# Pair 1 of the row tiles by seven products, begun while Y's signed sums are still being made

## The chip, the cores and the metric

The kernel runs on one core of one Trainium2 chip. The metric is device time in microseconds, the median of three runs. A TensorE program, a VectorE, a ScalarE and a GpSimd program and a queue of transfers (SP, called the transfer queue below) run side by side and wait for one another through semaphores.

## What is computed

`x` has 4096 rows of 512, `adj` is a 4096 by 4096 matrix of zeros and ones. Two layers follow one another, each with a residual and a layer norm:

```python
x = _layernorm(x + _L0_gnn_ref(x, key, value, adj, ...))   # attention, masked by adj, over 4096 keys
x = _layernorm(x + _L1_gnn_ref(x, adj, W, b))

def _L1_gnn_ref(features, adj, W, b):
    agg = adj @ features
    out = jnp.einsum('nd,od->no', agg, W) + b
    return jax.nn.relu(out)
```

The first layer takes four fifths of the time and is not changed. The kernel reorders the second: it first makes Y = x1 W^T (4096 by 512, x1 the first layer's result) and then adj @ Y. Every fp32 number on TensorE is split into two fp16 halves, HI and LO; `adj` is exact in bf16, so adj @ Y needs two matmuls for each 128x128 block of `adj`, one with Y's HI and one with its LO.

## The kernel before

**Y.** The first layer finishes one tile of 128 rows at a time. `rows_product(n)` (TensorE, 12 matmuls, line 952) makes tile n of Y. It needs the turned x1 tile `x1T`, two transposing transfers from the transfer queue (L542, L545). Tiles 0 to 27 of Y go through DRAM and are loaded into the large tile `Y` by GpSimd's queue; the last four are written to it by ScalarE and VectorE (`last_y_high`, `last_y_low`).

**Row tiles by pairs.** The 32 row tiles of the output are made in 16 pairs: pair p is row tile p and row tile p + 16. For each, both strips of `adj` are brought in, transposed, as `AT[p % 2][0]` and `AT[p % 2][1]` (32 blocks of 128x128 each). For pairs 0 and 1 a strip comes in four parts (`adj_part`, L563), for the later ones at once (`adj_tile`, L569). `at_in[h][k]` counts the parts that have landed.

**Plain pairs and pairs by seven products.** Pairs below `PLAIN` = 2 are made plainly by `aggregate(p, k, m0, m1)` (L1024): 32 blocks times HI and LO, 64 matmuls of 512 columns for each strip, 128 for a pair, with the accumulator in PSUM bank `2 * (p % 2) + k`. The other 14 pairs see the pair as a 2 by 2 block matrix (strip k, left or right half of the 4096 columns), Y as 2 by 2 (upper or lower half of the rows, left or right 256 columns), and multiply them by Winograd's scheme of seven products instead of eight. `product` (L1057) is 16 matmuls of 512 columns (256 columns, HI and LO side by side), so a pair costs 7 x 16 = 112.

The scheme needs sums of both factors. VectorE makes four sums of the `adj` strips for each pair, `adj_sum(0..3)` (L2107, tiles `S12`, `S34`, semaphore `s_comb`); sum 0 is the sum of the two halves of strip 1, so it waits for both strips. The signed sums of Y are the same for all pairs (tiles `Ta`, `Tb`, 16 groups of four): groups 0 to 10 (`EARLY` = 11) are made during the second pass of the first layer, stored in DRAM as `ts_dram` and loaded at the end by GpSimd's queue (L782, semaphores `ts_ld`, 5.5 MB in three transfers). Groups 11 to 15 need the last tiles of Y and are made at the end by VectorE and ScalarE: `joined(m)` (L2031) adds HI and LO, `last_sums(m)` (L1823 to L1828) makes the four sums, `signed_high(m)` (ScalarE, L1391) and `signed_low(m)` (L2042) split them; `t_lo2` counts the groups that are complete.

**After the products.** VectorE adds the seven products up in eleven steps (`taken`, `together`, L2114 and L2119, semaphore `c_step`), then `output` (L2062 scales and adds the bias, L2066 takes the relu and adds the x1 tile `zf`, L2069 takes statistics) and `result` (the root, L1783 to L1792, and L2078), and GpSimd's queue stores the tile. ScalarE copies product 0 out of its bank. TensorE waits in `seven` for `c_step` of the pair before (`read`), since each product has one bank: 0, 1, 2, 3, 6, 5, 4.

**The order around the change.** It is written out by hand. TensorE interleaves the last `rows_product` calls with pieces of `aggregate(0, ...)` and `aggregate(1, 0, 0, 8)`, then finishes pair 0, then pair 1, and goes on with `seven` for pair 2. VectorE makes the groups 11 to 15, then the outputs of tiles (0,0), (0,1), (1,0), then the four `adj` sums of pair 2, then the output of (1,1). The transfer queue issues in this order: `x1T` of tile 31, the four parts of strip `AT[1][1]`, the two `zf` tiles of pair 0 (L682), and when pair 0 is aggregated the two strips of pair 2 (L569).

Of the kernel before, what the change touches and what calls it, by code (L numbers as in the profile page):

```python
# [50 lines left out]
def attention_then_aggregation(nc, x, x_t, adj, key_t0, key_t1, value, wq, bq, wk, bk, wv, bv, wm_t, bm, w1, b1, out):  # L51
# [3 lines left out]
    P = 128  # L55
    KD = D // P
    NT = N // P
# [9 lines left out]
    PLAIN = 2  # L67
# [26 lines left out]
    with ctx:  # L94
# [278 lines left out]
        with nc.Block() as block:  # L373

            @block.sync
            def _(sp):
# [312 lines left out]
                for p in range(NP):  # L689
                    if p + 2 < NP:  # L690

                        q = p - PLAIN
                        if q < 0:
                            sp.wait_ge(f_mm, 2 * (p + 1))
                        else:
                            sp.wait_ge(s_prod, 7 * q + 6)
                            sp.wait_ge(s_comb, 4 * (q + 1))
                        for k in range(2):
                            adj_tile(p + 2, k)
                    if p + 1 < NP:  # L700
                        for k in range(2):
                            load_row(p + 1, k)
# [112 lines left out]
            def _(pe):  # L815
# [195 lines left out]

                def aggregate(p, k, m0, m1):

                    bank = 2 * (p % 2) + k
# [27 lines left out]
                aggregate(1, 0, 0, 8)  # L1042
# [7 lines left out]
                aggregate(1, 0, 8, NT)  # L1050
                aggregate(1, 1, 0, NT)

                def product(bank, left, right):
                    for m in range(NP):
                        last = nc.tensor.matmul(ps[:, bank, :].rearrange("p (s d) -> p s d", s=2), left(m), right(m),  # L1057
                                                start=(m == 0), stop=(m == NP - 1))
                    last.then_inc(s_prod, 1)

                def upper(h):
                    return lambda m: Y[:, m, :, h * H:(h + 1) * H]

                def lower(h):
                    return lambda m: Y[:, NP + m, :, h * H:(h + 1) * H]

                def signed(i):
                    return lambda m: (Ta, Tb)[m // PT2][:, m % PT2, i, :, :]

                def adj_block(h, k, half):  # L1070
                    return lambda m: AT[h][k][:, NP * half + m, :]

                def adj_sum(i):
                    return lambda m: (S12, S34)[i // 2][:, i % 2, m * P:(m + 1) * P]

                def seven(q, h, turn):
                    def read(step):

                        if not isinstance(q, int) or q > 0:
                            pe.wait_ge(c_step, 11 * (q - 1) + step)  # L1080

                    def plain_out(bank):

                        if isinstance(q, int) and q == 0:
                            pe.wait_ge(f_out, bank + 1)

                    pe.wait_ge(at_in[h][0], 16 * (turn + PARTS))
                    if not isinstance(q, int) or q > 0:
                        pe.wait_ge(s_cp, q)
                    plain_out(0)  # L1090
                    product(0, adj_block(h, 0, 0), upper(0))
                    read(1)
                    plain_out(1)
                    product(1, adj_block(h, 0, 1), lower(0))
                    pe.wait_ge(s_comb, 4 * q + 1)
                    if isinstance(q, int) and q == 0:
                        for c in range(3):
                            pe.wait_ge(ts_ld[c], 16)
                        pe.wait_ge(t_lo2, NP)
                    read(4)  # L1100
                    plain_out(2)
# [3 lines left out]
                    plain_out(3)  # L1105
# [10 lines left out]

                for p in range(PLAIN, PLAIN + 2):
                    seven(p - PLAIN, p % 2, p // 2)
# [303 lines left out]
            def _(dve):  # L1422
# [636 lines left out]
                def output(u, k, src, stored):  # L2059
# [3 lines left out]
                                                   op0=ALU.mult, op1=ALU.add).then_inc(f_out, 1)  # L2063
                    dve.wait_ge(zf_in[k], 16 * (stored + 1))
# [16 lines left out]
                def plain_output(p, k):  # L2081
                    u = 2 * p + k
                    dve.wait_ge(f_mm, u + 1)
                    output(u, k, ps[:, 2 * (p % 2) + k, :], p)
                    result(u, k)

                dve.wait_ge(s_bm, 32)
                plain_output(0, 0)
                plain_output(0, 1)
                plain_output(1, 0)  # L2090
# [3 lines left out]
                def adj_sum(i, q, h, turn):  # L2094
# [8 lines left out]
                    if q is not None:  # L2103
                        dve.wait_ge(s_prod, 7 * q + used)
# [4 lines left out]
                for i in range(4):  # L2109
                    adj_sum(i, None, PLAIN % 2, PLAIN // 2)  # L2110
                plain_output(1, 1)
# [10 lines left out]
                def pair(q, h, turn, nxt):  # L2122
# [9 lines left out]
                    dve.wait_ge(s_prod, 7 * q + 4)  # L2132
# [5 lines left out]
                    dve.wait_ge(s_prod, 7 * q + 5)  # L2138
# [4 lines left out]
                    dve.wait_ge(s_prod, 7 * q + 6)  # L2143
# [4 lines left out]
                    output(u, 1, cs[:, 1, :], q + PLAIN)  # L2148
# [3 lines left out]
                    dve.wait_ge(s_prod, 7 * q + 7)  # L2152
# [3 lines left out]
                    output(u + 1, 0, cs[:, 0, :], q + PLAIN)  # L2156
# [4 lines left out]
                for p in range(PLAIN, PLAIN + 2):  # L2161
                    pair(p - PLAIN, p % 2, p // 2, ((p + 1) % 2, (p + 1) // 2))
# [111 lines left out]
```

## Time and profile before

| what | value |
|---|---|
| median of 3 runs | 2019.56 us (2019.53 to 2020.5) |
| the profiled execution's own time | 2023.72 us |
| its span, first to last instruction | 2022.1 us |
| TensorE busy, of the span | 2003.9 us, 99% |
| VectorE busy | 1457.9 us, 72% |
| ScalarE busy | 689.6 us, 34% |
| mean granted TensorE clock | 0.999 |
| matmuls | 9273 |

The profiled execution is one execution under the hardware profiler, with a time of its own. Times within it are counted from the first instruction. The stretch that the change touches lies between about 1629 us and 1700 us. In a row of the timeline, the first number is the start, the second the time from there to the end of the last instruction of the row. Matmuls overlap, so the length of a row of n matmuls is longer than n times their distance; distances are taken from one start to the next.

### The profile page before, as it was taken

What the parts mean: (1) busy time and instruction counts of PE and PEld (TensorE: products, weight loads), DVE (VectorE), ACT (ScalarE), POOL (GpSimd) and SP (SyncE); (2) the same over time, 40 slices, a digit from 0 to 9 for tenths busy, and PEclk for the clock granted to TensorE, in tenths of its full rate; (3) what the DMA queues carried; (4) which work ended last, traced back from release to release, by engine and by line L of the source; (5) the groups of instructions that cost most, each with busy time, mean ns of one, the idle gap of its engine ahead of it and who ended that gap; (6) DMA issues with size and microseconds to landing.
All of it is one profiled execution on the core that took longest, in us unless ns stands there. A gap on an engine that the chain in (4) does not pass through costs nothing.

```text
span 2022.1 us, 29159 instructions
## 1 busy us (share of the span) xinstructions
PE 2003.9 (99%) x9273; PEld 920.8 (46%) x9273; DVE 1457.9 (72%) x3378; ACT 689.6 (34%) x859; POOL 72.1 (4%) x127
## 2 busy tenths in 40 slices
PE   8999999999999999999999999999999999999998
PEld 6444444444444444444444444444444444444443
DVE  7875666656666666777777777788888658788887
ACT  6854343434444443433333333344443210000000
POOL 0100000000000000000000000000000000000000
PEclk9999999999999999999999999999999999999999
DMA  8667778677777778877766676677777996555551
GB/s 296 229 167 157 202 176 207 151 157 166 179 175 176 187 165 206 197 165 167 166 162 161 164 166 161 164 168 178 182 184 208 220 274 146 125 128 137 133 134 60
DMA packets 566263, 351.22 MB, mean 174 GB/s; under 512 B 483520, under 2 KB 487616, under 8 KB 564288
## 3 DMA queue, kind: packets, MB, share of 16 engines
q1 hardware_dynamic: 548416, 279.26, 55.3%
q0 software_dynamic: 17792, 71.31, 15.3%
q8 instruction: 25, 0.41, 0.1%
q14 instruction: 30, 0.25, 0.0%
HBM read 176.95 MB, written 88.60 MB: 131 GB/s over the span
## 4 chain that ended last, share of the span: by engine, by line
PE 97%; SPq 1%; DVE 1%; DMA 1%; ACT 1%; issue 0%; DVEq 0%; ACTq 0%
PE ps L917 32%; PE ps L897 32%; PE ps L1057 17%; PE ps L874 4%; PE ps L952 4%; PE ps L938 4%; PE ps L1024 2%; PE ps L831 1%; SPq L563 1%; PE ps L849 1%; PE ps L819 0%; DMA PT<-Phl 0%; ACT prob L1243 0%; DVE prob L1685 0%; SPq L426 0%
## 5 line engine op out<-in xcount | busy, mean ns | idle before, releaser
L917 PE MATMUL ps<-V,PT 128*128 128x512 f16 x3072 | 673.5, 379 | 1.8 <-issue 1.4
L897 PE MATMUL ps<-KT,thl 128*128 128x512 f16 x3072 | 673.1, 379 | 0.0
L917 PEld LDWEIGHTS ps<-V,PT 128*128 128x128 f16 x3072 | 300.5, 98 | 364.6 <-issue 2.7
L897 PEld LDWEIGHTS ps<-KT,thl 128*128 128x128 f16 x3072 | 300.6, 98 | 362.1
L1672 DVE SCALAR_TENSOR_TENSOR prob<-ps,c_now,adjh 128x512 f32<-128x512 f32 x256 | 191.8, 750 | 264.1 <-PE ps L897 262.6
L1238 ACT ACTIVATE small<-prob 128x512 f32<-128x512 f32 x256 | 161.1, 630 | 621.1 <-DVE prob L1672 335.7
L1701 DVE SCALAR_TENSOR_TENSOR Phl<-prob,Phl 128x2048 f16<-128x2048 f32 x64 | 146.6, 2290 | 73.4 <-ACT Phl L1251 73.2
L1685 DVE CUSTOM_DVE_ANT_0 prob<-prob,small 128x512 f32<-128x512 f32 x256 | 174.2, 682 | 0.0
L1243 ACT ACTIVATE prob<-prob,nbias,inv 128x2048 f32<-128x2048 f32 x64 | 134.0, 2095 | 98.1 <-DVE nbias L1694 98.1
L1678 DVE TENSOR_SCALAR small<-small,eps_s,neg_s 128x512 f32<-128x512 f32 x256 | 138.7, 542 | 20.7 <-ACT small L1238 20.6
L1251 ACT ACTIVATE Phl<-prob 128x2048 f16<-128x2048 f32 x64 | 122.3, 1910 | 7.1
L1414 ACT ACTIVATE p<-ps 128x512 f32<-128x512 f32 x14 | 8.4, 597 | 323.5 <-PE ps L1057 323.5
L1057 PE MATMUL ps<-Y,AT 128*128 128x512 f16 x448 | 99.0, 379 | 0.0
L938 PE MATMUL ps<-Wvm,UT 128*128 128x512 f16 x384 | 88.1, 379 | 1.6 <-DMA UT<-Uhl 1.6
L952 PE MATMUL ps<-W1T,x1T 128*128 128x512 f16 x384 | 88.1, 379 | 0.2 <-DMA x1T<-x1hl 0.2
L758 POOL DMA_DIRECT2D adjh<-in_adj x64 | 36.8, 575 | 1364.3 <-DMA adj_bf<-adjh 701.1
L874 PE MATMUL ps<-xT,Aq 128*128 128x512 f16 x384 | 84.0, 379 | 0.0
L1057 PE MATMUL ps<-Ta,S 128*128 128x512 f16 x336 | 79.4, 379 | 0.0
L1057 PE MATMUL ps<-Tb,S 128*128 128x512 f16 x336 | 79.4, 379 | 0.0
L1057 PEld LDWEIGHTS ps<-Y,AT 128*128 128x128 bf16 x448 | 43.8, 98 | 52.9
L938 PEld LDWEIGHTS ps<-Wvm,UT 128*128 128x128 f16 x384 | 37.5, 98 | 47.2 <-DMA UT<-Uhl 2.1
L952 PEld LDWEIGHTS ps<-W1T,x1T 128*128 128x128 f16 x384 | 37.4, 98 | 46.1 <-DMA x1T<-x1hl 1.2
(205 smaller groups left out, 1677.3 us busy)
## 6 DMA issues: line engine op xcount, KB each, us to landing
adjh<-in_adj POOLq DMA_DIRECT2D x64, 512.0 KB, 5.3
adj_bf<-adjh SPq DMA_DIRECT2D x64, 512.0 KB, 4.7
t_in<-t_dram SPq DMA_DIRECT2D x64, 256.0 KB, 3.4
x_in<-in_x SPq DMA_DIRECT2D x64, 256.0 KB, 4.6
xraw<-in_x_t SPq DMA_DIRECT2D x8, 1024.0 KB, 7.3
t_dram<-tq POOLq DMA_DIRECT2D x8, 1024.0 KB, 5.5
o_dram<-z_out SPq DMA_DIRECT2D x32, 256.0 KB, 2.8
o_in<-o_dram SPq DMA_DIRECT2D x32, 256.0 KB, 4.5
```

The lines of the kernel that those rows point to most:

```text
L874: last = nc.tensor.matmul(ps[:, BT + e, :], Aq[:, m, k, e * P:(e + 1) * P], xT[:, b, s, k, :], start=(n == 0), stop=(n == 3 * KD - 1))
L897: last = nc.tensor.matmul(ps[:, BS + c, :], thl[:, b, s, k * P:(k + 1) * P], KT[:, m, k, c * C:(c + 1) * C], start=(n == 0), stop=(n == 3 ...
L917: last = nc.tensor.matmul(ps[:, BU + b, :], PT[:, b, s, m, :], V[:, v, m, :], start=(m == 0 and q == 0), stop=(m == MT - 1 and q == 2))
L938: last = nc.tensor.matmul(ps[:, BZ, :], UT[:, b, s, k, :], Wvm[:, m, k, :], start=(n == 0), stop=(n == 3 * KD - 1))
L952: last = nc.tensor.matmul(ps[:, BY, :].rearrange("p (o n) -> p o n", n=P), x1T[:, s, k, :], W1T[:, m, :, k, :], start=(q == 0), stop=(q == ...
L1057: last = nc.tensor.matmul(ps[:, bank, :].rearrange("p (s d) -> p s d", s=2), left(m), right(m), start=(m == 0), stop=(m == NP - 1))
L1238: nc.scalar.activation(small[:, c % 2, :], prob[:, b, c * C:(c + 1) * C], ACT.Abs).then_inc(s_abs, 1)
L1243: nc.scalar.activation(prob[:, b, :], prob[:, b, :], ACT.Exp, bias=nbias[:, b:b + 1], scale=inv[:, half:half + 1], accum_out=rsum[:, b:b + ...
L1672: nc.vector.scalar_tensor_tensor(out=prob[:, b, c * C:(c + 1) * C], in0=ps[:, BS + c, :], scalar=c_now[:, b:b + 1], in1=adjh[:, b, c * C:( ...
L1678: nc.vector.tensor_scalar(small[:, c % 2, :], small[:, c % 2, :], eps_s[:, half:half + 1], neg_s[:, half:half + 1], ALU.is_lt, ALU.mult).t ...
L1685: nc.vector.tensor_tensor_reduce(out=prob[:, b, c * C:(c + 1) * C], in0=prob[:, b, c * C:(c + 1) * C], in1=small[:, c % 2, :], scale=1.0, ...
L1701: nc.vector.scalar_tensor_tensor(out=Phl[:, b, LO, :], in0=prob[:, b, :], scalar=P_SCALE, in1=Phl[:, b, HI, :], op0=ALU.mult, op1=ALU.subt ...
```

## The change

`PLAIN` becomes 1, so pair 1 is made by seven products too, with an order of its own, and the other pairs keep theirs. On TensorE `aggregate(1, ...)` is gone. In its place stand product 0 of pair 1 (its first 8 matmuls ahead of the last `rows_product`), product 1, then product 4 (sum 3 of the strips times the lower part of Y), none of which needs Y's signed sums, then groups 0 to 10 of products 2, 3, 6 and 5, and at last groups 11 to 15 of the same four. Pair 0 now accumulates in banks 2 and 3. On VectorE the `adj` sums of pair 1 and the first step of pair 0's outputs (`take`, the bias step, which frees the banks) come between group 13 and group 14 of Y's sums, and the rest of pair 0's outputs after group 15. The transfer queue's instructions are the same; the third wait of its loop over pairs is another one.

```diff
-    PLAIN = 2
+    PLAIN = 1
...
-                            sp.wait_ge(s_prod, 7 * q + 6)
+                            sp.wait_ge(s_prod, 7 * q + (7 if q == 0 else 6))
...
-                    bank = 2 * (p % 2) + k
+                    bank = 2 + k
...
-                aggregate(1, 0, 0, 8)
+
+                pe.wait_ge(at_in[1][0], 16 * PARTS)
+                product(0, adj_block(1, 0, 0), upper(0), 0, NP // 2)
                 rows_product(NT - 1)
...
-                aggregate(1, 0, 8, NT)
-                aggregate(1, 1, 0, NT)
...
+                product(0, adj_block(1, 0, 0), upper(0), NP // 2, NP)
+                product(1, adj_block(1, 0, 1), lower(0))
+                pe.wait_ge(s_comb, 3)
+                pe.wait_ge(u_mg, NT)
+                product(4, adj_sum(3), lower(1))
+                for c in range(3):
+                    pe.wait_ge(ts_ld[c], 16)
+
+                pe.wait_ge(f_out, 1)
+                product(2, adj_sum(0), signed(0), 0, EARLY)
+                pe.wait_ge(f_out, 2)
+                product(3, adj_sum(1), signed(1), 0, EARLY)
+                pe.wait_ge(s_comb, 4)
+                pe.wait_ge(s_z, NT)
+                product(6, adj_sum(2), signed(2), 0, EARLY)
+                pe.wait_ge(at_in[1][1], 16 * PARTS)
+                product(5, adj_block(1, 1, 1), signed(3), 0, EARLY)
+                pe.wait_ge(t_lo2, NP)
+                product(2, adj_sum(0), signed(0), EARLY, NP)
+                product(3, adj_sum(1), signed(1), EARLY, NP)
+                product(6, adj_sum(2), signed(2), EARLY, NP)
+                product(5, adj_block(1, 1, 1), signed(3), EARLY, NP)
...
-                for m in range(EARLY + 2, NP):
-                    joined(m)
-                    signed_low(m - 2)
-                    last_sums(m)
-                signed_low(NP - 2)
-                signed_low(NP - 1)
...
+                joined(EARLY + 2)
+                signed_low(EARLY)
+                last_sums(EARLY + 2)
+                for i in (0, 1, 3, 2):
+                    adj_sum(i, None, PLAIN % 2, PLAIN // 2)
+                dve.wait_ge(s_bm, 32)
+                for k in range(2):
+                    dve.wait_ge(f_mm, k + 1)
+                    take(k, ps[:, 2 + k, :], 0)
+                for m in range(EARLY + 3, NP):
+                    joined(m)
+                    signed_low(m - 2)
+                    last_sums(m)
+                signed_low(NP - 2)
+                signed_low(NP - 1)
+                for k in range(2):
+                    output(k, k, 0)
+                    result(k, k)
```

Here `adj_sum(i, ...)` with i = 0 waits for both strips, `at_in[1][0]` and `at_in[1][1]`, before it starts. In the step that combines the products of pair 1 the counts of `s_prod` are moved by one (`made_at`), since product 4 is made third.

TensorE, the end of pair 0 and pair 1. Before, 16 matmuls of `aggregate(1, 0)` stand ahead of the last Y product and the other 112 of pair 1 behind pair 0's (the last 64 of them, strip 1, are the first two rows here); the products of pair 2 follow:

```order
L1024 MATMUL ps<-Y,AT 128x512 [waits adj_pair1_tile1_in]
L1024 MATMUL ps<-Y,AT 128x512 x63
L1057 MATMUL ps<-Y,AT 128x512 [waits aggregate_out,adj_pair0_tile0_in]
L1057 MATMUL ps<-Y,AT 128x512 x15
L1057 MATMUL ps<-Y,AT 128x512 [waits aggregate_out]
```

Now (S is a sum of the `adj` strips, Ta and Tb are Y's signed sums, `adj_sum_made` is `s_comb`):

```order
L1016 MATMUL ps<-Y,AT 128x512 x24
L1016 MATMUL ps<-Y,S 128x512 [waits halves_merged,adj_sum_made]
L1016 MATMUL ps<-Y,S 128x512 x15
L1016 MATMUL ps<-Ta,S 128x512 [waits signed_sums_loaded2,aggregate_out,signed_sums_loaded1,signed_sums_loaded0]
L1016 MATMUL ps<-Ta,S 128x512 x7
L1016 MATMUL ps<-Tb,S 128x512 x3
L1016 MATMUL ps<-Ta,S 128x512 [waits aggregate_out]
```

Only 24 matmuls now stand between the end of pair 0 and the first matmul that waits for a sum of the strips.

VectorE, behind group 13 of Y's signed sums (Yr and Tf are its stages). Before, group 14 follows at once:

```order
L1828 TENSOR_TENSOR Tf<-Tf,Yr 128x256 [waits signed_sums_made]
L2031 TENSOR_TENSOR Yr<-Y 128x512 [waits keys_then_y_in3]
L2031 TENSOR_TENSOR Yr<-Y 128x512 [waits y_lo]
L2042 TENSOR_TENSOR Tb<-Tf,Tb 128x4x256 [waits signed_sums_hi]
L1823 TENSOR_TENSOR Tf<-Yr 128x256 [waits signed_sums_lo,y_joined]
```

Now:

```order
L1838 TENSOR_TENSOR Tf<-Tf,Yr 128x256 [waits signed_sums_made]
L2107 TENSOR_TENSOR S<-AT 128x2048 [waits adj_pair1_tile1_in,adj_pair1_tile0_in]
L2107 TENSOR_TENSOR S<-S,AT 128x2048 [waits adj_sum_made]
L2107 TENSOR_TENSOR S<-AT,S 128x2048 [waits adj_sum_made]
L2107 TENSOR_TENSOR S<-AT 128x2048
L2066 SCALAR_TENSOR_TENSOR y<-ps,inv_y,b_rep 128x512 [waits aggregate_made,bm_then_b1_in]
L2066 SCALAR_TENSOR_TENSOR y<-ps,inv_y,b_rep 128x512 [waits aggregate_made]
L2041 TENSOR_TENSOR Yr<-Y 128x512 [waits keys_then_y_in3]
```

Four sums of the strips and two bias steps moved ahead of groups 14 and 15, and the first of them waits for both strips of pair 1.

## Rows read from the trace of the kernel before

**Rows 1.** The page: busy times, granted clock in 40 slices, last chain by engine.
```profile
PE 2003.9 (99%) x9273; PEld 920.8 (46%) x9273; DVE 1457.9 (72%) x3378; ACT 689.6 (34%) x859; POOL 72.1 (4%) x127
...
PEclk9999999999999999999999999999999999999999
...
PE 97%; SPq 1%; DVE 1%; DMA 1%; ACT 1%; issue 0%; DVEq 0%; ACTq 0%
```

**Rows 2.** The chain of waits from 1640 us: start, us, what.
```profile
1640.80 34.53 PE ps L1024 x160
1675.33 338.44 PE ps L1057 x1568
```

**Rows 3.** Timeline of TensorE: start, us, line, instruction, tiles, count.
```profile
1638.05 2.75 PE L952 MATMUL ps<-W1T,x1T 128*128 128x512 f16 x12
1640.64 34.70 PE L1024 MATMUL ps<-Y,AT 128*128 128x512 f16 x160
1675.17 7.07 PE L1057 MATMUL ps<-Y,AT 128*128 128x512 f16 x32
```

**Rows 4.** Tile AT, issues at 1640 us: durations ns; starts; time to landing.
```profile
L563 SPq DMA_TRANSPOSE AT<-adj_bf x1: 5229/5229/5229, 1639.6 to 1639.6; - x1
...
DMA to landing us min/median/max: 19.2/19.2/19.2
```

**Rows 5.** Busy time by window: PE, PEld, DVE, ACT, POOL, clock, DMA share, GB/s.
```profile
1637.00:1659.00 22.00, 22.00 (x104) 9.94 (x103) 16.14 (x30) 4.71 (x5) 1.62 (x3) 1.00 1.02 336
```

**Rows 6.** Timeline of the transfer queue.
```profile
1655.57 11.00 SPq L569 DMA_TRANSPOSE AT<-adj_bf  x2
```

**Rows 7.** Timeline of VectorE, 1652 to 1668 us; in brackets the idle time before.
```profile
1652.72 1.28 DVE L2031 TENSOR_TENSOR Yr<-Y 128x512 f32<-128x512 f16 x2
...
1656.72 1.28 DVE L2031 TENSOR_TENSOR Yr<-Y 128x512 f32<-128x512 f16 x2
...
1660.71 2.43 DVE L2042 TENSOR_TENSOR Tb<-Tf,Tb 128x1024 f16<-128x1024 f32 x2
1663.06 0.74 DVE L2062 SCALAR_TENSOR_TENSOR y<-ps,inv_y,b_rep 128x512 f32<-128x512 f32 x1
1663.90 0.69 DVE L2066 SCALAR_TENSOR_TENSOR y<-y,zf 128x512 f32<-128x512 f32 x1
...
1667.95 0.75 DVE L2062 SCALAR_TENSOR_TENSOR y<-ps,inv_y,b_rep 128x512 f32<-128x512 f32 x1
```

**Rows 8.** Timeline of VectorE, the sums of the strips of pair 2.
```profile
1677.73 1.22 DVE L2107 TENSOR_TENSOR S<-AT 128x2048 bf16<-128x2048 bf16 x1
1678.98 1.22 DVE L2107 TENSOR_TENSOR S<-S,AT 128x2048 bf16<-128x2048 bf16 x1
1680.12 1.22 DVE L2107 TENSOR_TENSOR S<-AT 128x2048 bf16<-128x2048 bf16 x1
```

**Rows 9.** Tile x1T, both transfers of tile 31: durations ns; starts; time to landing.
```profile
L545 SPq DMA_TRANSPOSE x1T<-x1hl x1: 1366/1366/1366, 1631.1 to 1631.1; - x1
...
DMA to landing us min/median/max: 6.4/6.9/7.4
```

**Rows 10.** Timeline of GpSimd: its wait for the same two transfers.
```profile
1637.82 0.55 POOL L782 DMA_DIRECT2D Ta<-ts_dram  x1 [9.02 <-DMA x1T<-x1hl]
```

**Rows 11.** Timeline of TensorE at the start of the program.
```profile
6.19 13.27 PE L831 MATMUL ps<-wk_s,wq_s 128*128 128x512 f32 x48 [6.19 <-DVE wk_s L1425]
19.30 2.88 PE L819 MATMUL ps<-wk_s,brep 128*128 128x512 f32 x12
22.02 2.88 PE L819 MATMUL ps<-wq_s,brep 128*128 128x512 f32 x12
```

**Rows 12.** Who waited for whom, TensorE, whole span: us, times, longest.
```profile
PE ps L938 <- DMA UT<-Uhl: 1.6, 1, 1.6
```

**Rows 13.** Timeline of VectorE, combining the products of pair 2.
```profile
1687.64 0.68 DVE L2114 TENSOR_TENSOR csum<-p,ps 128x512 f32<-128x512 f32 x1
...
1691.56 0.68 DVE L2114 TENSOR_TENSOR u<-u,ps 128x512 f32<-128x512 f32 x1
...
1699.58 1.22 DVE L2107 TENSOR_TENSOR S<-AT 128x2048 bf16<-128x2048 bf16 x1
```

More of the change, by code:

```diff
@@ L1010, in _, with product, upper, lower @@
                         project(g - 2, b, NT // 2 + i - 1)
+                def product(bank, left, right, m0=0, m1=NP):
+                    for m in range(m0, m1):
+                        last = nc.tensor.matmul(ps[:, bank, :].rearrange("p (s d) -> p s d", s=2), left(m), right(m),
+                                                start=(m == 0), stop=(m == NP - 1))
+                    if m1 == NP:
+                        last.then_inc(s_prod, 1)
+                def upper(h):
+                    return lambda m: Y[:, m, :, h * H:(h + 1) * H]
+                def lower(h):
+                    return lambda m: Y[:, NP + m, :, h * H:(h + 1) * H]
+                def signed(i):
+                    return lambda m: (Ta, Tb)[m // PT2][:, m % PT2, i, :, :]
+                def adj_block(h, k, half):
+                    return lambda m: AT[h][k][:, NP * half + m, :]
+                def adj_sum(i):
+                    return lambda m: (S12, S34)[i // 2][:, i % 2, m * P:(m + 1) * P]
                 def aggregate(p, k, m0, m1):
-                    bank = 2 * (p % 2) + k
+                    bank = 2 + k
                     if m0 == 0:
@@ L1049, in _ @@
                     aggregate(0, k, NT - 1, NT)
-                aggregate(1, 0, 8, NT)
-                aggregate(1, 1, 0, NT)
[L1055 to L1074, printed above, removed]
+                product(0, adj_block(1, 0, 0), upper(0), NP // 2, NP)
@@ L1076, in seven @@
                 def seven(q, h, turn):
                     def read(step):
[L1079 to L1085, printed above, removed]
+                        pe.wait_ge(c_step, 11 * (q - 1) + step)
                     pe.wait_ge(at_in[h][0], 16 * (turn + PARTS))
-                    if not isinstance(q, int) or q > 0:
-                        pe.wait_ge(s_cp, q)
@@ L1090, in seven @@
-                    plain_out(0)
+                    pe.wait_ge(s_cp, q)
                     product(0, adj_block(h, 0, 0), upper(0))
                     read(1)
-                    plain_out(1)
                     product(1, adj_block(h, 0, 1), lower(0))
                     pe.wait_ge(s_comb, 4 * q + 1)
[L1096 to L1099, printed above, removed]
@@ L1115, in seven @@
                     product(4, adj_sum(3), lower(1))
-                for p in range(PLAIN, PLAIN + 2):
+                for p in range(PLAIN + 1, 4):
                     seven(p - PLAIN, p % 2, p // 2)
```

36 lines of the change are left out of this document (14 added, 22 removed).

## The prediction, made before the changed kernel ran

> **What bounds the kernel now.** I read the page first: TensorE is busy for 99% of the span and makes 97% of the chain that ended last, VectorE is busy for 72% [rows 1]. So matmuls are the time, and the reader should then look where the changed stretch lies in the chain. From 1640.80 us it is 160 matmuls of `aggregate` and then 1568 of `product` without a single piece of another engine between them [rows 2]: TensorE waits for nobody there, and each matmul taken out is worth its whole distance. That distance is 338.44 / 1568 = 0.2158 us. It also means that any wait set between them is paid in full, so the second question, for which I read the timelines and the landing times of the transfers, is when the things that pair 1 will now need are there. In the kernel before pair 1 needs little and late: strip 1 at 1675.17 - 64 x 0.2158 = 1661.4 us, and neither a sum of the strips nor a signed sum of Y [rows 3].
>
> **The saving.** Pair 1 falls from 128 to 112 matmuls, all of 512 columns: 16 x 0.2158 = 3.45 us. Nothing else on the path is taken away. VectorE's work is the same in kind, with four strip sums (4 x 1.22 us) and the combining steps of one more pair; the 13 pairs that follow run without a wait of TensorE before [rows 2], so there is cover for that. 3.45 us is 0.17% of the time: the largest gain that the change can bring.
>
> **First wait: tile 31's `x1T`.** Product 0's part ahead of the last `rows_product` has 8 matmuls where 16 stood, so TensorE comes there 8 x 0.2158 = 1.73 us earlier, at 1638.05 - 1.73 = 1636.3 us [rows 3]. The second of the two transfers was issued at 1631.1 and landed 6.4 us later, at 1637.5 (the other at 1629.7 + 7.4 = 1637.1); GpSimd, which waited for the same two, went on at 1637.82 [rows 9, 10]. Before, these matmuls began just after. So TensorE now waits 1.2 to 1.5 us, I take 1.3; the 48 matmuls of pair 0 that follow start at 1640.25 instead of 1640.64 [rows 3].
>
> **Second wait: the strip sums.** Behind these 48 stand 24 matmuls of pair 1 (the rest of product 0, and product 1). TensorE is through at 1640.25 + 72 x 0.2158 = 1655.8 us and then needs three of the four strip sums (`s_comb` 3) for product 4. VectorE is ready for them at about 1652.3: the place of the first is that of group 14 of Y's sums, which stood at 1652.72 [rows 7], and the chain into it starts with the last Y product, which ends 0.4 us earlier. But the first sum adds the two halves of strip 1, so it waits for `AT[1][1]`. The last part of that strip was issued at 1639.6 us and took 19.2 us to land [rows 4], to 1658.8 us. Nothing of the change moves it: the transfer queue issues the same instructions in this stretch, and GpSimd's loads of Y's signed sums, issued at the same signal, run beside it; in this window all the transfer engines are full (share 1.02, 336 GB/s [rows 5]). The kernel before had covered it with pair 1's first strip. From the landing the sums follow one another at 1.25 us where one waits for the one before, 1.14 where not [rows 8]: the third is there after 1.25 + 1.25 + 1.22 + 0.05 for the semaphores = 3.8 us, at 1662.6. TensorE waits 1662.6 - 1655.8 = 6.8 us. VectorE stands idle for 6.5 of them, though groups 14 and 15 could be made meanwhile.
>
> The bounds of this term: not under 0, if the strip landed before VectorE asks (then sums end at 1656.1 and 0.3 us stay, which I round to nothing); upward I add the 5.2 us for which the queue held that one issue [rows 4], a measure of how far a full queue can set a transfer back: 12. I take 6.8, the row's own landing.
>
> **The clock.** TensorE now stands still for 6.8 us. At the start of the program it had stood for 6.19 us, and its first 48 matmuls took 19.30 - 6.19 = 13.11 us, 0.273 each, where the 12 after them took 2.72, 0.227 each [rows 11]: 13.11 - 48 x 0.227 = 2.2 us lost, though the page shows the granted clock as full in that slice too [rows 1]. The longest wait in the middle of the program is 1.6 us [rows 12]; the page's clock is full there. So the price lies between 0 and 2.2 us (or somewhat above). The new gap is as long as the one at the start, and I take 2.2.
> The Trainium skill, "TensorE: Matmul & The Clock Gate", section "HAM oscillation — how this bites in real kernels", says that a TensorE that waits long enough between bursts of matmuls falls to half its clock (1.2 of 2.4 GHz) and has to work for a while before it gets it back. The pace at the start agrees with it; no row of this trace shows it in the middle of a program. Without that rule the sum would be made with 0 here.
>
> **The rest of pair 1.** After 1662.6 come 16 + 44 matmuls, 12.95 us, and then groups 11 to 15, which need `t_lo2` = 16. VectorE makes the fourth strip sum, two bias steps (about 0.66 each behind one another), then two groups at 4.00 us and the two last splits at 2.35 [rows 7]: 6.1 + 8.0 + 2.4 = 16.5 us behind the landing, at 1675.4. TensorE is there at 1662.6 + 12.95 = 1675.5, or 2.2 later with the clock: no wait, but with nothing to spare. The loads of Y's signed sums must have landed before VectorE's bias steps end; they are issued at 1637.8 and after, and were needed at 1675.17 + 32 x 0.2158 = 1682.1 before [rows 3]. I cost them at nothing, since strip 1 shares the engines with them. 20 matmuls later pair 1 ends: 1662.6 + 80 x 0.2158 + 2.2 = 1682.1 us, against 1675.17 before [rows 3].
>
> **Pair 2.** Its early products wait for steps of pair 1's combination, and VectorE comes to these only after the outputs of both tiles of pair 0, 4.05 us each (1663.90 to 1667.95 [rows 7]): at 1675.4 + 8.1 = 1683.5. Product 1 of pair 2 needs the first step, 0.7 us later, at 1684.2; TensorE is there at 1682.1 + 3.45 = 1685.6. Product 2 needs the fourth, 3.92 + 0.7 later (1687.64 to 1691.56 [rows 13]), at 1688.1; TensorE: 1689.0. Product 6 needs strip sum 2, begun 1699.58 - 1687.64 = 11.9 us after the first step, and 1.2 long, so ready at the latest at 1683.5 + 13.1 = 1696.6, and some 2 us earlier without the waits for TensorE that lie in these 11.9; TensorE: 1695.9. I take all as covered, by about 1 us. Without the clock's 2.2 us, the first two are not, and cost 0.9 and 0.5 us. Strips of pair 2 are issued at 1655.57 as before [rows 6], so they are early; those of pair 3 some 7 us later than before, with a pair's time of cover. VectorE is free for over 3 us of each later pair and catches up; the end of the program is the same work.
>
> **The sum.** -3.45 + 1.3 + 6.8 + 2.2 = +6.9 us, which is also 1682.1 - 1675.2. The first wait is no loss by itself, since the second one ends at a fixed time and would be 1.3 us longer without it. Profiled time 2023.72 + 6.9 = 2030.6; as the median of runs, which lies 4.2 us lower and is the same program, 2019.56 + 6.9 = 2026.5 us.
>
> **Rivals.**
> *A, the forecast*: strip 1 is late, and the clock falls: 2026.5, own range 2025 to 2028. Chance 0.50.
> *B, the strip is late but the clock holds*: +4.65 at the end of pair 1, and the two waits of pair 2 that are then open, 0.9 + 0.5: +6.0, so 2025.6. For it: the page shows a full clock even at the start. Against it: the pace there. 0.22.
> *C, not slower: the strip lands in time.* What decides is the landing of the last part of `AT[1][1]`: from 1652.3 us on each microsecond later is a microsecond of TensorE's. At 1652.3 the sum is -3.45 + 1.3 + 0.9 + 0.5 = -0.7, so 2018.8. For it: the landing is read from one execution, under the profiler, and `x1T`'s transfers took a third as long shortly before [rows 9]. Against it: the full engines [rows 5]. With landings between (a wait of 1 to 4 us, sum 0 to +4): 0.20 together.
> *D, longer*: the landing is later still, or the clock's loss comes twice (at both waits), or pair 2 waits for VectorE as well: +9 to +12, 2029 to 2031. 0.08.
> That the change takes no matmuls out can be excluded: products 0 to 6 of pair 1 are 112.
>
> **How the numbers follow.** A measurement of this kernel tells about 0.2%, 4.0 us, from no change. Faster by that would need more than all 3.45 us: 0.03 for what I have overlooked. Slower by over 4.0: A and D whole, B nearly, 0.02 of C: 0.76, which I lower to 0.73. Within: 0.24. The range reaches from a short wait in C (+1.0) to the lower part of D (+9.9): 2020.6 to 2029.5.
>
> **What would show it.** Right: matmuls 9257; an idle time of about 1.3 us ahead of the last 12 matmuls on `x1T`, put down to that transfer; one of 6 to 7 us ahead of the first matmul `ps<-Y,S`, put down to VectorE's strip sums; on VectorE 6 to 7 us idle ahead of the first strip sum, released by the transfer of `AT`; then ten or more matmuls at twice the distance; pair 2 begins near 1682 us and the products from there to the end have the old distance. Wrong: no idle ahead of the strip sums (C); full pace right behind the gap (B); or idle of TensorE on `c_step` in pair 3 and after, which would make VectorE the bound.

## The result, and the profile after

| | before | after |
|---|---|---|
| median | 2020.5 us (2019.53 to 2022.85, 7 runs) | 2028.27 us (2026.42 to 2028.85, 7 runs) |
| ratio, 95% interval | 1 | 1.0035 (1.0026 to 1.0044) |
| the profiled execution's own time | 2023.72 us | 2028.27 us |
| its span | 2022.1 us | 2026.6 us |
| matmuls | 9273 | 9257 |
| mean granted clock | 0.999 | 0.996 |

The kernel became slower by 0.35%, 7.1 us by the ratio (the two medians lie 7.8 apart), though 16 matmuls are gone. Where the time went is seen first in the list of waits of TensorE (engine, tile and line <- who ended the wait: us, times, longest), after:

```profile
PE ps L1016 <- DVE S L2107: 6.8, 1, 6.8
PE ps L831 <- DVE wk_s L1435: 6.3, 1, 6.3
PE ps L952 <- DMA x1T<-x1hl: 2.0, 2, 1.8
```

The second row was there before [rows 11]; the first is new, and the third was 0.2 us before. Both stand in the timeline of TensorE, after, which answers to [rows 3]:

```profile
1622.98 2.76 PE L952 MATMUL ps<-W1T,x1T 128*128 128x512 f16 x12 [0.22 <-DMA x1T<-x1hl]
...
1634.42 2.76 PE L952 MATMUL ps<-W1T,x1T 128*128 128x512 f16 x12 [1.77 <-DMA x1T<-x1hl]
1637.02 10.52 PE L1048 MATMUL ps<-Y,AT 128*128 128x512 f16 x48
1647.38 5.34 PE L1016 MATMUL ps<-Y,AT 128*128 128x512 f16 x24
1659.53 6.50 PE L1016 MATMUL ps<-Y,S 128*128 128x512 f16 x16 [6.81 <-DVE S L2107]
1665.87 1.89 PE L1016 MATMUL ps<-Ta,S 128*128 128x512 f16 x8
...
1679.69 7.07 PE L1016 MATMUL ps<-Y,AT 128*128 128x512 f16 x32
...
1703.86 7.07 PE L1016 MATMUL ps<-Y,AT 128*128 128x512 f16 x32
```

The 24 matmuls end at 1652.72 us, and product 4 starts at 1659.53: the wait of 6.81 us. Then its 16 matmuls take 1665.87 - 1659.53 = 6.34 us where 16 took 3.45. Pair 2 starts at 1679.69, pair 3 at 1703.86, 24.17 us later, which is 112 matmuls at 0.2158 and no wait.

The two profiled executions were already 3.8 us apart when the changed stretch began (the Y product of tile 30 starts at 1622.98 now, at 1626.81 before), so their spans, 4.5 us apart, are not the measure. This start differs from one execution to the next: in the eight experiments below it lies between 1622.51 and 1626.75. Here and in all experiments I measure the *stretch*: from the start of the Y product of tile 30 to the first matmul of pair 3. These are the rows of the kernel before, TensorE's timeline:

```profile
1626.81 2.76 PE L952 MATMUL ps<-W1T,x1T 128*128 128x512 f16 x12 [0.24 <-DMA x1T<-x1hl]
...
1699.34 7.07 PE L1057 MATMUL ps<-Y,AT 128*128 128x512 f16 x32
```

Before it is 1699.34 - 1626.81 = 72.53 us, after 1703.86 - 1622.98 = 80.88: +8.35. What ended the long wait is in the timeline of VectorE, after, where [rows 7] stood:

```profile
1655.73 1.23 DVE L2107 TENSOR_TENSOR S<-AT 128x2048 bf16<-128x2048 bf16 x1 [6.54 <-DMA AT<-adj_bf]
...
1658.25 1.22 DVE L2107 TENSOR_TENSOR S<-AT,S 128x2048 bf16<-128x2048 bf16 x1
```

and in the chain of waits, after (start, us, what), which ran through TensorE alone in [rows 2] and now goes through the transfer of strip 1:

```profile
1636.72 18.92 DMA AT<-adj_bf
...
1659.53 358.76 PE ps L1016 x1648
```

The last part of `AT[1][1]` took 18.9 us from issue to landing, as 19.2 in [rows 4]. The clock is read from a table of windows, after (window, its length, busy time and count of PE, PEld, DVE, ACT and POOL, granted clock, DMA share, GB/s):

```profile
1653.00:1655.00 2.00, 0.00 (x0) 0.00 (x0) 0.00 (x0) 0.00 (x0) 0.00 (x0) 1.00 1.23 209
1655.00:1656.00 1.00, 0.00 (x0) 0.00 (x0) 0.27 (x1) 0.00 (x0) 0.00 (x0) 0.58 1.08 371
1656.00:1659.50 3.50, 0.00 (x0) 0.00 (x0) 3.43 (x4) 0.00 (x0) 0.00 (x0) 0.50 1.24 298
1659.53:1665.87 6.34, 6.34 (x16) 2.29 (x17) 6.20 (x11) 0.00 (x0) 0.00 (x0) 0.54 0.90 189
1666.00:1679.00 13.00, 13.00 (x62) 5.86 (x60) 12.16 (x31) 2.56 (x3) 0.55 (x1) 1.00 0.18 43
```

The granted clock falls to 0.50, the lower of its two levels, 1.2 of 2.4 GHz, while TensorE stands still, and nearly all of the 16 matmuls run at it. This agrees with the Trainium skill, "TensorE: Matmul & The Clock Gate", section "HAM oscillation — how this bites in real kernels", as the prediction gave it, and now a row in the middle of the program shows it.

### The profile page after: what moved, and what is told of

Read it like the earlier page. It is cut to its first block, busy times and chain, and to the rows that moved or that the text cites. A ratio compares the mean times of both kernels' runs of the same rounds, so it can differ in the third digit from the quotient of the medians.

```text
span 2026.6 us, 29160 instructions
## 1 busy us (share of the span) xinstructions
PE 2002.9 (99%) x9257; PEld 918.2 (45%) x9257; DVE 1468.4 (72%) x3393; ACT 690.2 (34%) x860; POOL 71.8 (4%) x127
## 4 chain that ended last, share of the span: by engine, by line
PE 97%; SPq 1%; DMA 1%; DVE 1%; issue 0%; ACT 0%; DVEq 0%
PE ps L917 33%; PE ps L897 33%; PE ps L1016 18%; PE ps L874 4%; PE ps L952 4%; PE ps L938 4%; DMA AT<-adj_bf 1%; SPq L563 1%; PE ps L831 1%; PE ps L849 1%; PE ps L819 0%; SPq L542 0%; DVE S L2107 0%; DMA wb<-in_Wk 0%; DMA x1T<-x1hl 0%; SPq L545 0%
## 5 line engine op out<-in xcount | busy, mean ns | idle before, releaser
L1016 PE MATMUL ps<-Y,AT 128*128 128x512 f16 x480 | 106.2, 379 | 0.0
L1016 PE MATMUL ps<-Tb,S 128*128 128x512 f16 x360 | 85.2, 379 | 0.0
L1016 PE MATMUL ps<-Ta,S 128*128 128x512 f16 x360 | 85.0, 379 | 0.0
L1016 PE MATMUL ps<-Y,S 128*128 128x512 f16 x240 | 57.1, 394 | 6.8 <-DVE S L2107 6.8
```

## The experiments

All are edits of the changed kernel, and each ratio is against the kernel before in the same job (2021.48 us beside fill28, whole0, g14_first and sums_gated, 2021.03 beside gate_third, gated_groups and best2). The theory at the start: the loss is the landing of strip 1 behind the strip sums, plus the clock that falls in the gap, and the landing is late because GpSimd's loads from `ts_dram` (5.5 MB) share the transfer engines with it. Its rivals: the pace of the 16 matmuls has another cause than idleness; the first wait, on `x1T`, adds to the loss; VectorE's order of work makes it; seven products with their later needs cost more than they save whatever the transfers do.

### fill28: the gap filled with matmuls

```diff
                 product(1, adj_block(1, 0, 1), lower(0))
+                pe.wait_ge(y_lo, NT)
+                for m in range(28):
+                    nc.tensor.matmul(ps[:, BY, :], AT[1][0][:, m, :], Y[:, m % NP, HI, :], start=(m == 0), stop=(m == 27))
                 pe.wait_ge(s_comb, 3)
```

> The changed kernel with 28 matmuls of no use (512 columns, strip 0 times Y's HI, into PSUM bank 7, which nobody reads) put where TensorE waits for the strip sums: 28 x 0.2158 = 6.04 us of work in a gap of 6.8 to 7.0 us. Theory (the gap has two prices, the wait itself and, behind it, half the clock: 16 matmuls took 6.34 instead of 3.45 us): the wait stays where it ends, the 16 matmuls take 3.45 us, the kernel is 2.9 us faster than the changed one, so +5.4 against before instead of +8.3 in the trace. Rival 1 (the matmuls behind the gap are slow for another reason, such as the reading of the strip sums or the full transfer engines): they stay at 6.3 us, no gain. Rival 2 (the gap is not a fixed end but work that the fill delays): slower by up to 6 us.

Measured: 2026.56 us, ratio 1.0028 (1.0017 to 1.004). TensorE's timeline, fill28:

```profile
1651.81 6.21 PE L1082 MATMUL ps<-Y,AT 128*128 128x512 f16 x28
1658.56 3.63 PE L1016 MATMUL ps<-Y,S 128*128 128x512 f16 x16 [0.54 <-DVE S L2110]
1662.02 1.89 PE L1016 MATMUL ps<-Ta,S 128*128 128x512 f16 x8
...
1675.83 3.62 PE L1016 MATMUL ps<-Y,AT 128*128 128x512 f16 x16
1680.02 3.63 PE L1016 MATMUL ps<-Y,AT 128*128 128x512 f16 x16 [0.57 <-DVE csum L2132]
1684.03 1.89 PE L1016 MATMUL ps<-Ta,S 128*128 128x512 f16 x8 [0.39 <-DVE u L2132]
...
1698.17 3.63 PE L1016 MATMUL ps<-Y,S 128*128 128x512 f16 x16
1701.64 7.07 PE L1016 MATMUL ps<-Y,AT 128*128 128x512 f16 x32
```

The 16 matmuls take 3.46 us at a clock of 1.00. So it was the idleness that made them slow, and nothing in their operands. But pair 1 now ends earlier than VectorE can follow, and waits appear in pair 2, which starts at 1675.83: from there to pair 3 it is 25.81 us instead of 24.17, 1.64 lost. The stretch is 78.66 us, +6.13. Of the 2.9 us of the clock 1.6 come back as waits, which were hidden behind it. So the theory of the clock held and the sum of +5.4 did not: it left these waits out. The stretch is 2.22 us shorter than after's, of which 1.24 are the clock less the new waits, and 0.97 lie ahead of product 4, which starts 35.58 us behind tile 30's Y product instead of 36.55.

### whole0: no wait on x1T

```diff
                 product(0, adj_block(1, 0, 0), upper(0), 0, NP // 2)
+                for c in (2, 3):
+                    pe.wait_ge(*y_ld[c])
+                    product(0, adj_block(1, 0, 0), upper(0), c * TC, (c + 1) * TC)
                 rows_product(NT - 1)
...
-                product(0, adj_block(1, 0, 0), upper(0), NP // 2, NP)
```

(Each of the two last quarters of product 0 waits for its load of Y.)

> The changed kernel with all 16 matmuls of product 0 ahead of the last Y product, instead of 8. Theory (the wait for tile 31's x1T costs nothing by itself, since the strip sums end at a fixed time): the wait for x1T falls from 1.8 to under 0.3 us, the gap ahead of the first matmul on a strip sum grows from 7.0 to about 8.6, the time stays that of the changed kernel within 0.3 us. Rival (both waits add up, the first is a cost of its own): 1.5 to 1.9 us faster.

Measured: 2028.04 us, ratio 1.0034 (1.002 to 1.0049); the wait on `x1T` is 0 and the later one has grown. TensorE's timeline, whole0:

```profile
1660.24 5.60 PE L1016 MATMUL ps<-Y,S 128*128 128x512 f16 x16 [7.83 <-DVE S L2109]
1665.67 1.89 PE L1016 MATMUL ps<-Ta,S 128*128 128x512 f16 x8
```

The landing of `x1T` is where GpSimd goes on, first in whole0, then after:

```profile
1635.40 0.55 POOL L782 DMA_DIRECT2D Ta<-ts_dram  x1 [8.80 <-DMA x1T<-x1hl]
```
```profile
1634.66 0.55 POOL L782 DMA_DIRECT2D Ta<-ts_dram  x1 [9.69 <-DMA x1T<-x1hl]
```

From there to product 4 it is 24.84 us here and 24.87 after. Counted from this landing the first wait costs nothing: it only shortens the second. The stretch, 79.05 us, is 1.83 shorter than after's, and by this number alone the rival (1.5 to 1.9 us faster) would fit. But 0.91 of it is the clock's loss, which is smaller here (5.43 us for the 16 matmuls against 6.34), and 0.92 lie ahead of the landing of `x1T`. That part differs between executions of one order too: GpSimd goes on 11.68 us behind tile 30's Y product after, 10.93 in fill28, whose order up to there is the same, and 10.79 here. The times, with an interval of 3 us to each side, cannot tell the two.

### g14_first: VectorE uses its idle time

```diff
                 last_sums(EARLY + 2)
+                joined(EARLY + 3)
+                signed_low(EARLY + 1)
+                last_sums(EARLY + 3)
                 for i in (0, 1, 3, 2):
...
-                for m in range(EARLY + 3, NP):
+                for m in range(EARLY + 4, NP):
```

> The changed kernel with group 14 of Y's signed sums (4.0 us of VectorE) made ahead of the four strip sums, in the time in which VectorE stands idle for 6.5 us. Theory (only the landing of strip 1 decides when the strip sums end): VectorE's idle time falls to about 2.5 us, the gap of TensorE stays 6.8 to 7.0 us, Y's sums are complete 4 us earlier, and the time is unchanged within 0.3 us. Rival (VectorE's lost time is what makes the kernel slow, through the later steps of pairs 1 and 2): 2 to 4 us faster. Second rival (VectorE was ready only just before the landing, so its order matters): slower by up to 4 us.

Measured: 2027.57 us, ratio 1.0032 (1.0019 to 1.0044). VectorE's idle time ahead of the first strip sum falls from 6.54 to 2.38 us, and TensorE's wait stays. VectorE's timeline and TensorE's, g14_first:

```profile
1656.09 1.23 DVE L2107 TENSOR_TENSOR S<-AT 128x2048 bf16<-128x2048 bf16 x1 [2.38 <-DMA AT<-adj_bf]
```
```profile
1659.89 5.62 PE L1016 MATMUL ps<-Y,S 128*128 128x512 f16 x16 [6.65 <-DVE S L2107]
```

VectorE's order was not the cause; the landing of the strip sets both. The stretch, 79.70 us, is 1.18 shorter than after's, of which 0.88 are the clock's (5.46 us for the 16 matmuls against 6.34).

### sums_gated: the loads held back until the strip has landed

```diff
                 for c in range(2):
+                    if c == 0:
+                        pool.wait_ge(at_in[1][1], 16 * PARTS)
                     load_sums(c, Ta[:, 4 * c:4 * c + 4, :, :, :])
```

> The changed kernel with GpSimd's three loads of Y's stored signed sums (5.5 MB) held back until strip 1 of pair 1 has landed. Theory (these loads crowd the transfer engines and make the last two parts of the strip take 19 us): the parts land within 6 to 8 us of their issue, some 13 us earlier than now, the wait of VectorE for the strip is gone and TensorE's gap ahead of product 4 falls from 7.0 to under 0.5 us. The loads now end about 17 us behind the strip, so a new wait of 3 to 5 us stands ahead of product 2, for the last of them; 2 to 5 us faster than the changed kernel, depending on whether the clock falls there. Rival (the strip's transfers are slow of themselves, or behind others of their own queue): the strip lands as late as now, the loads later still, and the kernel becomes 8 us slower or more.

Measured: 2024.0 us, ratio 1.0009 (0.9999 to 1.0019). Issues and landing of the four parts of the strip, in the view of tile `AT` on the transfer queue, sums_gated:

```profile
L563 SPq DMA_TRANSPOSE AT<-adj_bf x4: 1323/1484/3222, 1633.3 to 1639.5; - x4
...
DMA to landing us min/median/max: 4.6/5.6/6.4
```

With the loads beside them the same four took, after:

```profile
L563 SPq DMA_TRANSPOSE AT<-adj_bf x4: 1337/2728/5479, 1629.8 to 1636.7; - x4
DMA to landing us min/median/max: 5.3/13.4/19.9
```

This is the cause of the late strip, shown by its removal: 6.4 us at most instead of 19.9. How the loads delay it is not shown. The share of the transfer engines, from which the prediction read that they were full [rows 5], does not tell the two cases apart; while the strip's parts come in without the loads, it is above 1 as well, and only the rate is lower (264 GB/s against 336). The window in sums_gated:

```profile
1633.30:1641.00 7.70, 6.60 (x32) 2.81 (x31) 0.68 (x2) 0.00 (x0) 0.00 (x0) 1.00 1.10 264
```

What the loads now cost is a new wait, as TensorE's timeline says, sums_gated:

```profile
1656.01 3.63 PE L1018 MATMUL ps<-Y,S 128*128 128x512 f16 x16 [0.18 <-DVE S L2109]
1662.17 1.89 PE L1018 MATMUL ps<-Ta,S 128*128 128x512 f16 x8 [2.53 <-DMA Tb<-ts_dram]
```

The stretch is 73.40 us, +0.87. That is 7.48 less than after's, and by the ratios of the times 5.3 less, more than the 2 to 5 us of the theory. In the gap of 2.53 us the clock stays at 1.00, and the matmuls behind it keep their distance of 0.2158 us. This is one execution, and not the rule: the granted clock averaged over a whole execution is 0.999 in it and in two more of the ten, and 0.997 or 0.998 in the other seven, while it is 0.999 in all ten of gated_groups below, where this gap is gone. So the clock probably fell behind it in most executions; no trace shows those.

### gate_third: only the last of the three loads held back

```diff
+                pool.wait_ge(at_in[1][1], 16 * PARTS)
                 load_sums(2, Tb[:, 0:EARLY - 8, :, :, :])
```

> The changed kernel with only the third load of Y's stored signed sums (1.5 of the 5.5 MB) held back until strip 1 has landed. Theory (the strip's landing follows the bytes that stand beside it: 1.5 MB at 336 GB/s are 4.5 us): the last part lands 14 to 15 us after its issue instead of 18.9, TensorE's gap ahead of product 4 falls from 7.0 to 2 to 3 us, and a gap of that length leaves the clock alone, so the 16 matmuls take 3.45 us. 4.5 + 2.9 us are saved, 1.3 come back ahead of products 1 and 2 of pair 2 as in the run with the filled gap: about 6 us faster than the changed kernel, +2 against before. Rival (the second load, issued right beside the first, already fills the engines, and a third one only queues up behind the two): the landing hardly moves, under 1 us gained, and the clock is lost as before.

Measured: 2024.07 us, ratio 1.0015 (1.0006 to 1.0025). TensorE's timeline and two windows, gate_third:

```profile
1656.62 6.58 PE L1017 MATMUL ps<-Y,S 128*128 128x512 f16 x16 [3.05 <-DVE S L2108]
1663.04 1.89 PE L1017 MATMUL ps<-Ta,S 128*128 128x512 f16 x8
```
```profile
1655.50:1656.60 1.10, 0.00 (x0) 0.00 (x0) 1.10 (x2) 0.00 (x0) 0.00 (x0) 0.64 1.28 290
1656.62:1663.04 6.42, 6.42 (x16) 2.33 (x17) 6.28 (x11) 0.00 (x0) 0.00 (x0) 0.53 1.12 364
```

Two loads beside the strip instead of three: the longest of the four landings is 16.1 us instead of 19.9, that of the last part 14.8 instead of 18.9, and the wait is 3.05 us instead of 6.81. So the landing comes earlier with fewer bytes beside it, as expected, and the rival is out. My expectation that the clock would be left alone was wrong: this short gap cost as much of it (6.42 - 3.45 = 2.97 us) as the long one. The profiled execution is the one with the lowest mean clock of the ten (0.997; eight have 0.998, one 0.999), so 2.97 is rather the most than the usual. The kernel is 4.4 us faster than the changed one in the stretch, where 6 were expected.

### gated_groups: the loads held back, and their groups taken as they come

Beside the edit of sums_gated, products 2, 3, 6 and 5 no longer wait for all three loads at once:

```diff
                 for c in range(3):
                     pe.wait_ge(ts_ld[c], 16)
-
-                pe.wait_ge(f_out, 1)
-                product(2, adj_sum(0), signed(0), 0, EARLY)
...
+                    m0, m1 = 4 * c, min(4 * c + 4, EARLY)
...
+                    product(2, adj_sum(0), signed(0), m0, m1)
...
+                    product(3, adj_sum(1), signed(1), m0, m1)
...
+                    product(6, adj_sum(2), signed(2), m0, m1)
...
+                    product(5, adj_block(1, 1, 1), signed(3), m0, m1)
```

> The kernel with all three loads held back, with the signed groups taken as they come: products 2, 3, 6 and 5 over groups 0 to 3, then over 4 to 7, then over 8 to 10, each behind its own load, so that the last load is needed 6.9 us later. Theory: the wait of 2.7 us for the last load goes; 2 of it are saved, since Y's signed sums of VectorE are complete 16.5 us after the strip sums begin and the tail then waits 0 to 0.3 us for them, and 1.3 us come ahead of products 1 and 2 of pair 2, where VectorE is late. So 1.2 to 1.8 us faster than with the loads held back alone, and -0.5 to 0 against before. Rival (the interleaving of four accumulations in short pieces costs matmul time): as slow as with the loads held back alone, or slower.

Measured: 2021.02 us, ratio 1.0 (0.9991 to 1.0009). TensorE's waits, gated_groups:

```profile
PE ps L954 <- DMA x1T<-x1hl: 1.3, 1, 1.3
PE ps L1018 <- DVE csum L2135: 0.6, 1, 0.6
PE ps L1018 <- DVE u L2135: 0.4, 1, 0.4
...
PE ps L1018 <- DVE S L2113: 0.2, 1, 0.2
```

No large wait is left in the stretch, and it is 72.51 us: as long as before. The 3.45 us are spent on the first wait (1.41 from start to start), which now is a loss since nothing late stands behind it, on 0.35 ahead of product 4, and on 1.66 in pair 2.

### best2: VectorE's order changed as well

Product 0 whole ahead of the last Y product, the strip sums ahead of group 13, the last five groups in two steps; and the second output of pair 0, `output(1, 1, 0)`, put off in pair 1's combination, behind strip sums 2 and 3 of pair 2:

```diff
                     taken(q, 4, u5[:, :], u2[:, :], ps[:, 2, :], ALU.add)
+                    first = isinstance(q, int) and q == 0
+                    if first:
+                        adj_sum(2, q, *nxt)
+                        adj_sum(3, q, *nxt)
...
+                    if first:
+                        output(1, 1, 0)
+                        result(1, 1)
                     dve.wait_ge(c_step, 11 * q + 9)
                     take(1, cs[:, 1, :], q + PLAIN)
```

> What the runs point to, in one kernel: loads held back until the strip has landed and taken as they come; all of product 0 ahead of the last Y product, so that no matmul waits for x1T; the strip sums ahead of group 13 of Y's signed sums instead of behind it; the tail split in groups 11 to 13 and 14 to 15; and in pair 1's combination the two last strip sums of pair 2 first and the second output of pair 0 behind step 9. Theory (every wait of this stretch is one of order): from the last Y product on TensorE waits for nothing, pair 1 takes its 112 matmuls, the saving of 3.45 us is seen whole: ratio to before 0.9983, the interval hardly clear of 1. Rival 1 (VectorE has too much to do in this stretch: strip sums, groups 11 to 15, outputs): 1 to 3 us of waits on it remain, ratio 0.999 to 1. Rival 2 (the saving is given back by later transfers, the strips of pair 3 being asked for late): a wait at the start of pair 3.

Measured: 2024.6 us, ratio 1.0018 (1.0009 to 1.0027): slower than gated_groups. VectorE's timeline and TensorE's, best2:

```profile
1688.64 0.75 DVE L2075 SCALAR_TENSOR_TENSOR y<-cs,inv_y,b_rep 128x512 f32<-128x512 f32 x1 [5.41 <-DMA out<-y]
```
```profile
1668.41 7.07 PE L1018 MATMUL ps<-Y,AT 128*128 128x512 f16 x32
...
1694.37 4.97 PE L1018 MATMUL ps<-Y,S 128*128 128x512 f16 x16 [5.08 <-DVE csum L2137]
1699.18 7.07 PE L1018 MATMUL ps<-Y,AT 128*128 128x512 f16 x32
```

Up to pair 2 most is gained, 2.97 of the 3.45 us: from tile 30's Y product it is 1668.41 - 1623.02 = 45.39 us, where before took 1675.17 - 1626.81 = 48.36. The rest is a wait of 0.34 us for a bias step ahead of product 2. Then the bias step directly behind the output put off needs the buffer `y` of the tile whose store has just been issued, waits for that transfer to land, and the steps that TensorE needs for product 4 are queued behind it. The wait of 5.08 us lowers the clock again (16 matmuls in 4.81 us, at a mean granted clock of 0.71). Neither the theory nor its rivals had this wait.

### best3: the same, with the store given time

```diff
                     taken(q, 4, u5[:, :], u2[:, :], ps[:, 2, :], ALU.add)
+                    first = isinstance(q, int) and q == 0
+                    if first:
+                        output(1, 1, 0)
+                        result(1, 1)
+                        adj_sum(2, q, *nxt)
+                        adj_sum(3, q, *nxt)
...
+                    if first:
+                        dve.wait_ge(s_prod, 7)
+                        taken(q, 10, csum[:, 1, :], u5[:, :], ps[:, 4, :], ALU.add)
+                        together(q, 10, 1, 0, 1)
                     dve.wait_ge(c_step, 11 * q + 9)
                     take(1, cs[:, 1, :], q + PLAIN)
```

(and both bias steps of pair 0 moved ahead of group 13, with the strip sums.)

> As gated_groups (the strip's loads ahead of those from ts_dram, the groups of 2, 3, 6 and 5 taken as each load lands), and VectorE's work put in another order: the strip sums and both take steps ahead of group 13, the last five groups in two steps, product 0 of pair 1 whole ahead of the last Y product, and in the combination of pair 1 the output and store of block (1,1) right behind u5, then sums 2 and 3 of pair 2, then the rest. Theory (the 3.45 us of the 16 matmuls are real, and the waits only gave them back): no wait of TensorE over 0.6 us between the last Y product and the end of pair 2, the store has landed before the take that needs its buffer, clock 1.00, from the start of rows_product(30) to pair 2's first matmul 45.0 to 45.6 us (before 48.36), and the time 3 to 4 us below before: ratio 0.998 to 0.9985. Rival 1, VectorE is still late in pair 2 or 3: waits of 1 to 3 us there, ratio 0.999 to 1.0. Rival 2, the take waits for the store again (about 5 us of TensorE and a lost clock): ratio 1.001 to 1.002.

Measured: 2018.19 us (11 runs) against 2020.84 of before in the same job, ratio 0.9987 (0.9978 to 0.9996): faster than before by about 2.6 us, with an interval of 0.8 to 4.4, and so faster than the changed kernel too. TensorE's waits and the stretch, best3:

```profile
PE ps L1018 <- DVE u L2137: 0.2, 1, 0.2
```
```profile
1622.51 2.76 PE L954 MATMUL ps<-W1T,x1T 128*128 128x512 f16 x12
...
1667.41 7.07 PE L1018 MATMUL ps<-Y,AT 128*128 128x512 f16 x32
...
1691.97 7.07 PE L1018 MATMUL ps<-Y,AT 128*128 128x512 f16 x32
```

To pair 2 it is 44.90 us, 3.46 less than before: 16 matmuls, all of them. To pair 3 it is 69.46, 3.07 less. In the profile the theory of that kernel holds against its rivals: the largest wait of the stretch is 0.22 us, and the seven products are worth nearly what they promise once nobody waits. The time gained less than the 3 to 4 us that were expected, and its ratio of 0.9987 lies between the theory's and rival 1's. What each of the edits that best3 adds to gated_groups is worth was not measured one by one.

### The profiles against the times

| kernel | wait for strip sums | the 16 matmuls of product 4 of pair 1 | lost in pair 2 | stretch, against 72.53 | by the ratio of the times (x 2020.5) |
|---|---|---|---|---|---|
| after | 6.81 | 6.34 | 0 | +8.35 | +7.1 |
| fill28 | 0.54 | 3.46 | 1.64 | +6.13 | +5.7 |
| whole0 | 7.83 | 5.43 | 0 | +6.52 | +6.9 |
| g14_first | 6.65 | 5.46 | 0 | +7.17 | +6.5 |
| gate_third | 3.05 | 6.42 | 0 | +3.92 | +3.0 |
| sums_gated | 0.18 | 3.46 | 0 | +0.87 | +1.8 |
| gated_groups | 0.18 | 3.46 | 1.66 | -0.02 | 0.0 |
| best2 | 0 | 3.45 | 6.60 | +3.63 | +3.6 |
| best3 | 0 | 3.45 | 0.39 | -3.07 | -2.6 |

One execution's stretch and the medians of many agree to 1.3 us. The intervals of the ratios are about 2 us to each side, so the differences among after, fill28, whole0 and g14_first are shown by their traces alone, not by their times.

## Why the prediction was right

It said 2026.5 us, slower; measured were 2028.27. That is just above the forecast's own range (A, 2025 to 2028) and inside the whole one. The forecast was counted from a median of three runs, 2019.56; from the 2020.5 of seven it is 2027.4. By its steps:

- **The saving, 3.45 us**: right, and seen alone in best3 (3.46).
- **The wait on `x1T`, 1.3 us**: 1.77 after, and 1.0 to 1.6 in the experiments that kept it. That it is no loss by itself was right while the strip is late (whole0), and it became one as soon as the strip was early (1.41 us in gated_groups).
- **The wait for the strip sums, 6.8 us**: 6.81. It came from a landing time that the kernel before had hidden. That nothing of the change would move it was right. That GpSimd's loads beside it make it late was shown by sums_gated. The engines' share of 1.02, which the prediction gave as the reason, does not show it: the share is 1.10 while the strip lands early.
- **The clock, 2.2 us**: the term that was mis-sized. It cost 6.34 - 3.45 = 2.89 us in the profile after, 1.98 in whole0, 2.01 in g14_first, 2.97 in gate_third. The term was read from the start of the program, and that it came so near is partly luck: from 6.19 to 19.30 us before, while the first 48 matmuls run, the granted clock is 1.00, so no row shows that their slow pace has to do with the clock, and its cause stays open. In the middle of the program the windows show 0.50 in the gap. Rival B, that the clock holds, is what fill28 makes, and its balance was good too: 6.0 forecast, 6.13 in fill28's stretch.
- **The rest of pair 1**: no wait was forecast, with nothing to spare. From 1665.87 to 1679.69 us 64 matmuls took 13.82, 0.2159 each. Right.
- **Pair 2**: covered with the clock lost, right; 0.9 + 0.5 us of waits without it. In fill28 they are 0.74 and 0.56 (starts of products 1 and 2 less 3.45), and 0.34 more that I had not forecast, 0.29 of it ahead of product 4.
- **The sum, +6.9 us**: +8.35 in the profiled stretch, +7.1 by the times. Of the 1.45 between forecast and profile 0.7 is the clock and 0.2 the second wait, which is 6.97 from start to start. 0.6 is the first: the last Y product starts 11.44 us behind tile 30's, 11.24 before, and with 8 matmuls fewer it should be 9.51, so it cost 1.93.

What the prediction did not see is that the same profile held the way out: the loads that make the strip late are needed only behind the strip sums, and run beside the strip that these wait for.

## What to carry to other kernels

A change that takes work off the bound engine pays only if all that the new order needs has landed by then: read the landing time of each such transfer in the kernel before, also where nobody waits for it, for it may be late and hidden. If it is late beside transfers that are needed later, hold those back and take them piece by piece. Here most waits that were removed uncovered another, and only the kernel with none over 0.22 us left in the stretch was faster than before.

## What the runs showed of the hardware

- The granted clock fell to 0.50 inside a gap of 6.8 us, and the 16 matmuls behind gaps of 6.65 to 7.83 us lost 2.0 to 2.9 us. A gap of 3.05 us lost 2.97, one of 2.53 us nothing, one of 5.08 us 1.36. These are single executions, and the loss does not grow with the gap in them; what decides it stays open. The mean clocks of the ten executions of sums_gated (0.997 to 0.999) say that it differs from one to the next.
- Four transposing transfers of one strip landed 4.6 to 6.4 us after their issue when alone, and 5.3 to 19.9 us beside 5.5 MB of loads from another queue. Holding back one of the three loads brought the longest to 16.1 us. The share of the transfer engines was above 1 with the loads (1.02) and without them (1.10).
- Loads issued after the strip had landed cost TensorE no wait in gated_groups, which takes the groups as they land, while waiting for all three cost 2.53 us in sums_gated.
